# The first layer's weights and the dense work of both batches in one phase, the second batch's projections between the first one's feed-forward jobs

## The reference

```
xn = layernorm(x)
Q, K, V = (xn @ W.T).reshape(b, 16, t, 16) for W in (Wq, Wk, Wv)   # a plain reshape: 64 tokens make one head
x = x + softmax_causal(Q @ K.T / 4) @ V @ Wp.T + bp
      + rms_norm(relu(xn @ ternary(W_fc).T) ** 2) @ ternary(W_proj).T
# ternary(w): w rounded to bfloat16, in groups of 64; scale = mean |w| of a group,
# q = clip(round(w / scale), -1, 1), result q * scale. W_fc is 1024 x 256, W_proj 256 x 1024.
```

## Time and profile before

| | us |
|---|---|
| median of 3 runs | 1415.71 |
| lowest, highest | 1410.51, 1415.78 |
| the profiled execution: its time | 1415.78 |
| the profiled execution: its span | 1414.0 |

### The profile page before, as it was taken

How to read it: one execution, slowest core, us unless ns; L and a number is a source line. 1 busy time by engine, 2 the same in 40 slices (tenths; PEclk the granted TensorE clock), 3 DMA queues, 4 the chain that set the end, 5 groups by cost and what they waited for, 6 DMA issues and landing times. The chain is left out here.

```text
span 1414.0 us, 22409 instructions
## 1 busy us (share of the span) xinstructions
PE 1207.6 (85%) x7424; PEld 863.5 (61%) x7424; DVE 880.8 (62%) x2323; ACT 736.7 (52%) x1683; POOL 515.6 (36%) x545
## 2 busy tenths in 40 slices
PE   2584936899999898888589999999999999999978
PEld 2474834444444386776467767676776776766667
DVE  7674637989999534544476666666766666666501
ACT  1461610677877615545266566665666656666400
POOL 0130323433442100505055554545555554555200
PEclk8796975889999997999789999999999999999989
DMA  2262737446650093210311110110111111110091
GB/s 89 56 128 64 115 89 79 55 56 100 97 61 24 1 256 123 64 39 0 96 27 41 42 42 21 49 31 28 41 42 42 41 42 42 27 31 16 16 314 58
DMA packets 111100, 91.50 MB, mean 65 GB/s; under 512 B 49488, under 2 KB 101136, under 8 KB 109200
## 3 DMA queue, kind: packets, MB, share of 16 engines
q1 hardware_dynamic: 109952, 89.10, 27.8%
q10 hardware_dynamic: 1040, 1.05, 0.2%
HBM read 51.05 MB, written 30.67 MB: 58 GB/s over the span
## 5 line engine op out<-in xcount | busy, mean ns | idle before, releaser
L775 POOL TENSOR_SCALAR a_p<-a_p,a_rl 128x128 f32<-128x128 f32 (+7 forms) x256 | 216.3, 846 | 346.1 <-DVE a_rl L717 346.0
L758 ACT ACTIVATE a_p<-psum,a_nm 128x128 f32<-128x128 f32 (+7 forms) x256 | 189.5, 740 | 112.0 <-DVE a_nm L711 111.6
L1261 ACT ACTIVATE a_pt<-psum 128x512 f32<-128x512 f32 (+3 forms) x384 | 167.6, 493 | 73.1 <-PE psum L1121 70.5
L808 PE MATMUL psum<-ident,a_p 128*128 128x128 f32 x1152 | 171.3, 276 | 22.5 <-DVE a_pt L744 20.0
L830 PE MATMUL psum<-a_pt,v 128*64 128x256 f32 (+1 forms) x1280 | 160.3, 372 | 0.6 <-ACT a_ot L844 0.6
L1111 PE MATMUL psum<-a_op_k,a_op_q 64*128 64x512 f32 (+3 forms) x384 | 135.2, 449 | 27.7 <-DVE a_op_k L1227 26.5
L808 PEld LDWEIGHTS psum<-ident,a_p 128*128 128x128 f32 x1152 | 129.4, 141 | 46.3 <-issue 39.2
L711 DVE CUSTOM_DVE_ANT_0 psum<-psum,mask_a 128x128 f32<-128x128 f32 (+3 forms) x128 | 63.4, 496 | 139.3 <-PE psum L793 139.2
L1121 PE MATMUL psum<-a_op_q,a_op_k 64*128 64x512 f32 (+3 forms) x384 | 127.4, 411 | 8.4 <-ACT a_pt L1261 7.2
L742 ACT ACTIVATE a_pt<-psum 128x256 f32<-128x256 f32 (+2 forms) x192 | 87.2, 454 | 88.0 <-PE psum L808 86.9
L1121 PEld LDWEIGHTS psum<-a_op_q,a_op_k 64*128 64x128 f32 x384 | 62.4, 192 | 102.0 <-ACT a_pt L1261 83.2
(11 more groups left out here) (313 smaller groups left out, 2775.9 us busy)
## 6 DMA issues: line engine op xcount, KB each, us to landing
a_swap<-w_p SPq DMA_DIRECT2D x64, 128.0 KB, 2.4
ot_d<-a_ot SPq DMA_DIRECT2D x16, 512.0 KB, 2.6
o_ot<-ot_d SPq DMA_DIRECT2D x8, 1024.0 KB, 8.7
a_raw_q<-qk_d SPq DMA_DIRECT2D x48, 128.0 KB, 4.3
room<-qk_d SPq DMA_DIRECT2D x48, 128.0 KB, 7.6
w<-wf_d SPq DMA_DIRECT2D x16, 384.0 KB, 3.4
qk_d<-p_stage_h SPq DMA_DIRECT2D x64, 64.0 KB, 2.0
qk_d<-p_stage_l SPq DMA_DIRECT2D x64, 64.0 KB, 2.0
```

The costliest lines, as they stand in the source:

```text
L758: e.activation(s.p[:, t % NPB, 0:(i + 1) * P], C.score[t % 2][:, 0:(i + 1) * P], ACT.Exp, scale=-1.0, bias=s.nm[:, k:k + 1], accum_out=s.l ...
L775: e.tensor_scalar(s.p[:, t % NPB, 0:(i + 1) * P], s.p[:, t % NPB, 0:(i + 1) * P], s.rl[:, k:k + 1], 1.0, ALU.mult, ALU.mult).then_inc(s.no ...
L808: ins = e.transpose(C.turn[par][:, (k - k0) * P:(k - k0 + 1) * P], s.p[:, tt % NPB, k * P:(k + 1) * P], C.ident[:, :])
L1261: e.activation(pt[:, k // G0 % NPT, hd, off:HALF], bank_b("score", g, k)[:, off:HALF], ACT.Exp, scale=-1.0).then_inc(exped, 1)
```

## The change

`weights0`, `project0`, `feed0` and the loop over the batches go. One function, `dense0`, does their work for both batches in one phase, with an order written out by hand for each engine:

- SyncE loads batch 0's x, then Wq, Wk, Wv, Wp, W_proj, batch 1's x and the bias. ScalarE's queue still issues W_fc.
- The projection jobs of a batch are ordered qk, qk, v, four times. Batch 0's twelve run without lifts; between them VectorE quantises W_fc in eight steps (`Quantised`: narrow, magnitude, limits (two), below, above, sign, scaled, which are the instructions of `ternary`) and takes batch 1's layer-norm statistics. The transposes of W_fc and Wp come after job 7, those of batch 1's rows after job 11.
- Then 12 slots hold batch 1's projection n and batch 0's lift n. VectorE quantises W_proj in slots 2 to 7. Its transposes and batch 0's first drop follow slot 11.
- Then batch 0's lifts 12 to 15 and batch 1's 16 lifts run, with the drops spread between them, one token tile after a lift. Batch 1's second drop ends the phase.
- The bias is added to x on GpSimd, ahead of all squares, instead of on VectorE. The stage of Q and K holds two groups of 128 rows instead of four, and the stage of V, one tile, serves both batches. The rounded tiles h_h and h_l have 12 rooms instead of 16. The ring tiles r, h and sq first hold the weights.
- Batch 0's norm and additions are done within batch 1's lifts.

The diff, cut to its core (`Turns` has the units of transposes with their waits, `Rows0` the layer norm's steps):

```diff
-def weights0(nc, C, W, Wq, Wk, Wv, Wp, Wfc, Wproj):
...
-def project0(ph, C, W, b, x_in, xt_h, xt_l, x, qk_d, v_d, bias, bp):
...
-def feed0(ph, C, W, before, b, xt_h, xt_l, x, bias, acc_d):
...
+class Quantised:
...
+    def below(self, e):
+        e.wait_ge(self.step, 4)
+        lim = self.limit[:, :].unsqueeze(2).to_broadcast(self.shape)
+        e.scalar_tensor_tensor(out=self.neg[:, :, :], in0=self.wb[:, :, :], scalar=-1.0, in1=lim,
+                               op0=ALU.mult, op1=ALU.is_gt).then_inc(self.step, 1)
+
...
+JOBS_P = [job for mt in range(4) for job in (("qk", mt, 0), ("qk", mt, 1), ("v", mt, None))]
+JOBS_F = [(c, m) for c in range(NCH) for m in range(NH0)]
+N_P, N_F = len(JOBS_P), len(JOBS_F)
+ROOMS_H = 12
...
+def dense0(nc, C, w_p, x_in, weights, bp, qk_d, v_d, acc_d):
...
+        stage_h, stage_l = (ph.sb(f"stage_{n}", [P, 2, T], F32R) for n in "hl")
+        stage_v = ph.sb("stage_v", [P, NT // 2, 2 * E])
+        h_h, h_l = (ph.sb(f"h_{n}", [P, ROOMS_H, HALF], F32R) for n in "hl")
...
+        wfc, wpr, qfc = flat_h, flat_r, flat_r
+        qpr = xn[:, :, :].rearrange("p t e -> p (t e)")
...
+                load_x(0)
...
+                load_x(1)
+                e.dma_start(bias[:, :], bp.rearrange("(a m) -> a m", a=1).to_broadcast([P, E])).then_inc(bias_in, 16)
+                for b in range(B):
+                    for mt in range(4):
+                        J = b * N_P + 3 * mt + 2
+                        e.wait_ge(p_high, J)
+                        e.wait_ge(p_low, b * 8 + 2 * mt + 2)
+                        for part, stage in ((0, stage_h), (1, stage_l)):
+                            for j in range(P // D0):
...
+                    e.wait_ge(p_high, (b + 1) * N_P)
+                    e.dma_start(v_d[b * T:(b + 1) * T, :].rearrange("(t p) m -> p t m", p=P),
+                                stage_v[:, :, :].rearrange("p c (t m) -> p (c t) m", m=E)).then_inc(v_stored, 16)
...
+            @block.tensor
...
+                def project(b, n):
+                    kind, mt, c = JOBS_P[n]
+                    J = b * N_P + n
+                    bank = p_banks[J % 2]
+                    if J >= 2:
+                        e.wait_ge(p_high, J - 1)
+                        old_b, old_n = divmod(J - 2, N_P)
+                        if JOBS_P[old_n][0] == "qk":
+                            e.wait_ge(p_low, old_b * LOWS_P[N_P] + LOWS_P[old_n + 1])
...
+                def drop(b, c, i):
+                    if i == 0:
+                        e.wait_ge(high, b * N_F + (c + 1) * NH0)
+                        e.wait_ge(low, b * N_F + (c + 1) * NH0)
+                        if b:
+                            e.wait_ge(added, 4 * (c + 1))
...
+                e.wait_ge(loaded, 64)
+                for u in U["qkv"]:
+                    turns.turn(e, u)
+                for u in U["rows0"]:
+                    e.wait_ge(rows[0].made, 4 * ((u - U["rows0"][0]) // KE + 1))
+                    turns.turn(e, u)
+                turns.taken(e, "rows0")
+                for n in range(N_P):
+                    project(0, n)
+                    if n == 7:
+                        e.wait_ge(fc.made, 1)
+                        for u in U["fc"]:
+                            turns.turn(e, u)
+                        e.wait_ge(padded, KE + 1)
+                        for u in U["wp"]:
+                            turns.turn(e, u)
+                for u in U["rows1"]:
+                    e.wait_ge(rows[1].made, 4 * ((u - U["rows1"][0]) // KE + 1))
+                    turns.turn(e, u)
+                turns.taken(e, "rows1")
+                for n in range(N_F):
+                    if n < N_P:
+                        project(1, n)
+                    lift(0, n)
+                    if n == N_P - 1:
+                        e.wait_ge(pr.made, 1)
+                        for u in U["pr"]:
+                            turns.turn(e, u)
+                        turns.taken(e, "pr")
+                        for i in range(4):
+                            drop(0, 0, i)
+                e.wait_ge(p_high, B * N_P)
+                e.wait_ge(p_low, B * LOWS_P[N_P])
+                square_sums(0, 0)
+                for n in range(N_F):
+                    lift(1, n)
+                    if n in (2, 3, 4, 5):
+                        drop(0, 1, n - 2)
+                    if n == 3:
+                        square_sums(0, 1)
+                    if n in (10, 11, 12, 13):
+                        drop(1, 0, n - 10)
+                    if n == 11:
+                        square_sums(1, 0)
+                drop(1, 1, 0)
+                square_sums(1, 1)
+                for i in range(1, 4):
+                    drop(1, 1, i)
+            @block.scalar
...
+                        if M >= 2:
+                            e.wait_ge(stored[M % 2], (M // 2) * 16 * 2 * (P // D0))
...
+                        if b:
+                            e.wait_ge(v_stored, 16 * b)
...
+                def round_h(N):
+                    e.wait_ge(squared, N + 1)
+                    if N >= ROOMS_H:
+                        e.wait_ge(down, dropped(N - ROOMS_H))
...
+                rows[0].root(e)
+                for u in [*U["qkv"], *U["rows0"]]:
+                    turns.round_high(e, u)
+                for n in range(N_P):
+                    project(0, n)
+                    if n == 7:
+                        for u in [*U["fc"], *U["wp"]]:
+                            turns.round_high(e, u)
+                    if n == 8:
+                        rows[1].root(e)
+                for u in U["rows1"]:
+                    turns.round_high(e, u)
+                for N in range(B * N_F):
+                    if N < N_P:
+                        project(1, N)
+                    cut(N)
+                    if N >= 2:
+                        round_h(N - 2)
+                    if N == N_P - 1:
+                        for u in U["pr"]:
+                            turns.round_high(e, u)
+                    if N == N_F + 5:
+                        mean_root(0)
+                for N in range(B * N_F - 2, B * N_F):
+                    round_h(N)
+                mean_root(1)
+            @block.gpsimd
+            def _(e):
+                def add_bias(b):
+                    e.wait_ge(rows[b].made, NT)
+                    for tt in range(NT):
+                        e.tensor_tensor(x[b][:, tt, :], x[b][:, tt, :], bias[:, :], ALU.add).then_inc(biased, 1)
+                e.wait_ge(bias_in, 16)
+                for b in range(B):
+                    add_bias(b)
...
+            @block.vector
...
+                for n in range(NT // 2):
+                    rows[0].count(e, n)
+                rows[0].variance(e)
+                rows[0].rows(e)
+                for u in [*U["qkv"], *U["rows0"]]:
+                    turns.keep_low(e, u)
+                fc.narrow(e)
+                pr.narrow(e)
+                project(0, 0)
+                fc.magnitude(e)
+                project(0, 1)
+                fc.limits(e)
+                fc.below(e)
+                fc.above(e)
+                project(0, 3)
+                fc.sign(e)
+                project(0, 4)
+                fc.scaled(e)
+                e.wait_ge(loaded, 64)
+                e.memset(wpp[:, :, :, :], 0.0).then_inc(padded, 1)
+                project(0, 6)
+                e.wait_ge(padded, 1)
+                for mt in range(KE):
+                    e.tensor_copy(wpp[:, mt, :, 0:D0], wp[:, mt, :].rearrange("p (h d) -> p h d", d=D0)).then_inc(padded, 1)
+                rows[1].count(e, 0)
+                rows[1].count(e, 1)
+                project(0, 7)
+                rows[1].count(e, 2)
+                rows[1].count(e, 3)
+                rows[1].variance(e)
+                project(0, 9)
+                turns.all_turned(e, "rows0")
+                rows[1].rows(e)
+                project(0, 10)
+                for u in U["rows1"]:
+                    turns.keep_low(e, u)
+                quantise = {2: pr.magnitude, 3: pr.limits, 4: pr.below, 5: pr.above, 6: pr.sign}
+                for N in range(B * N_F + 2):
+                    if N < N_P:
+                        project(1, N)
+                    if N >= 2:
+                        join(N - 2)
+                    if N in quantise:
+                        quantise[N](e)
+                    if N == 7:
+                        turns.all_turned(e, "rows1")
+                        pr.scaled(e)
+                    if N == N_F + 5:
+                        means(0)
+                    if N == N_F + 7:
+                        add(0)
+                means(1)
+                add(1)
...
-            with ExitStack() as dense:
...
-                bias = dsb("bias", [P, E])
-                with nc.Fori(0, B) as b:
-                    with Phase(nc, "d0", repeated=True) as ph:
```

(40 more changed lines are left out.)

527 lines of the change are left out of this document (241 added, 286 removed).

## The result

| | before | after |
|---|---|---|
| median, us | 1415.74 (4 runs) | 1394.65 (4 runs, 1392.24 to 1401.04) |
| profiled execution: time, span | 1415.78, 1414.0 | 1393.61, 1391.8 |
| mean granted clock | 0.923 | 0.937 |
| first instruction of the next phase | 203.22 | 184.30 |

The ratio is 0.9852, with an interval of 0.9816 to 0.9888: 1.5% faster. The forecast was 1385; its range held the time, and its own smaller range (1374 to 1395) just did. The profiled executions differ by 22.2 us: 18.9 of them lie ahead of the next phase, 3.3 behind it. Forecast were 30.4 and 0.

The account below looks back on a forecast made before the run. TensorE bounds only the slots; other stretches are chains through VectorE, GpSimd and DMA. Stage end points put the next phase at 172.8 instead of 203.2 us: 1415.78 less 30.4 gives 1385 us, range 1369 to 1401 (own 1374 to 1395).

Parts of the forecast that it names:

- Start: From phase start to the first projection, through loads, rows and transposes: 21.5 us, where it was 57.66 before.
- Batch 0's projections: Batch 0's projections beside W_fc's quantising, then batch 1's rows and transposes: to 55 us.
- V's wait: ScalarE at batch 1's first V job stands from 61 until batch 0's V store lands at 65.9: cost 4.9 us.
- Slots: Twelve slots, paced by VectorE without pause from the first join at 68.2, with 10.8 us of W_proj's steps: to 97.5.
- First drop: W_proj's transposes (3.66 us, plus 0.6 for ScalarE), then batch 0's first drop of 64 matmuls (7.54 us): to 109.3.
- Twenty lifts: Lifts with eight token tiles of drops, paced by GpSimd and VectorE at 2.1 us a unit: 50 us, to 159.3.
- End: Last drop at the lower clock 9.1 us, fourth powers 0.5, one addition 0.5, then 3.4 to the next phase: 172.8.
- Rival 1: In the lifts, squares fit beside VectorE's work and TensorE paces: 13.5 us less, 1372; chance 0.15.
- Rival 2: In the slots, Q/K and V stores on SyncE's queue pace through the two-group stage: +12 us, 1397; chance 0.16.
- Rival 3: From 21 us on, TensorE falls to the lower clock and stays there: +46 us, 1431, slower than before; chance 0.06.
- Rival 4: Time is moved, not saved: the next phase starts early but loses as much; within 0.5% of now; chance 0.03.
- three conditions under which I would be wrong: Lifts 1.8 us apart; ScalarE's Q/K store waits over 3 us in sum; lower clock in over half of 21 to 160 us.

Follow-up runs that it names:

- short quantising: Changed kernel with three of W_proj's quantising steps left out (both comparisons and their difference), so output differs: 1390.89 us, ratio 0.9831 to the kernel before.
- late drops: Changed kernel with the two drops between batch 1's lifts begun two lifts later, 14 rooms for h_h and h_l: 1390.2 us, ratio 0.9844 to the kernel before.

## Why the prediction was right in sign and 10 us short

**Start (21.5; measured 22.59), right.** The bias additions on GpSimd took 7.54 us for eight (0.94 each, beside the casts) and 5.54 (0.69 each): inside 0.5 to 1.0. One cast went from 1.22 to 1.77 us, the hindrance that I had put at 0.5.

**Batch 0's projections (55; measured 53.3, batch 1's first stage on ScalarE at 55.30), right.** The sum, the comparisons and the product took 2.27 to 2.29 us as read in the earlier trace rows, and VectorE had no wait over 0.2 us from 24 to 44 us. The one term left out is the stage's wait at 46.10, 1.20 us.

**V's wait (4.9; measured 5.63, ending at 66.00 where I had 65.9), right as a wait, not as a price.** Without it the first join came 6.3 us earlier, but join 9 only 3.5 and the phase's end 2.1. In the sum I priced it as if nothing were late behind it, though the store of Q and K was next in line, with waits of 3.46 and 1.44 us.

**Slots (first join 68.2, measured 67.64; end 97.5, measured 96.2 by the last matmul of lift 11), right, for the reason given.** VectorE has no idle from join 0 to join 8 and the short quantising shows that it paces. The rule that I weighed here (the Trainium skill, SBUF — State Buffer, section "SBUF: two separate sides") foresaw exclusion for the quantising too, at +2 us. Part of that is seen: a square begun beside a comparison took 1.96 or 2.50 us instead of 1.04, and one beside the product 1.78. But the comparison kept its 2.28, so GpSimd paid and VectorE, which paces, did not:

```profile
80.49 2.28 DVE L400 TENSOR_TENSOR d_wb_pr<-d_wb_pr,d_limit_pr 128x2048 bf16<-128x2048 bf16 x1
...
81.17 2.50 POOL L717 TENSOR_TENSOR d_h<-d_r 128x512 f32<-128x512 f32 x1 [1.15 <-ACT d_r L657]
```

Beside the sum, which has one input, the square kept its 1.04 (69.17).

**First drop (to 109.3; measured 107.8, the next low part at 109.92), right.** The 16 transposes ran at the full clock, 1.91 us for my 3.66, and ScalarE's rounding behind them took TensorE 1.92 us for my 0.6.

**Twenty lifts (50; measured 61.7, 107.8 to 169.5), wrong, and this is the step that failed.** The failed term is "2 for the lifts held back behind a drop that waits for the eighth low part". The terms for VectorE and GpSimd were right and somewhat high: from join 10 on VectorE is busy for 41.0 of 59.6 us (2.05 a unit where the pair is closed, 1.20 where the squares were made before) against 46.4 for them and the norm. Its idle time is 18.6 us instead of 2. I priced the wait by its length on one engine. But it is a round trip: behind the low part waited for, VectorE has one more join, and the next unit is rounded only behind a ReLU whose lift stands behind the token tile. So the other engines run dry while TensorE catches up on a whole tile, cold. The two waits cost about 9 us (late drops: 8.9 less idle). At the full clock, in the same order, they would cost 4.1 less (matmuls ahead of the drops: 2.87 and 2.83 instead of 4.57 and 5.20). Most of the other 9.7 is TensorE's 2.83 us a unit, larger than the pair's 2.1. I had TensorE's 35.2 us and the pair's 44.4 as two totals and took the larger; stage by stage the larger one changes.

**End (13.5 from the last low part; measured 14.8, 169.5 to 184.30), about right.** It ran cold as forecast, behind 5.95 us of idle TensorE. Of the eight additions two were left for the end, not one: 0.88 us at 180.34.

**Behind the phase (0; measured −3.3).** Nothing there was changed. The attention phase took 288.8 us against 288.5, and the difference came in the dense phase after it. The two spread by 6.6 and 6.4 us between executions of kernels that share them, so no cause is named. It hides a part of the miss by luck: the phase ended 11.5 us later than forecast, the profiled execution 8.2.

**The rivals.** Rival 1 (the pair doesn't pace) fell: 2.05 us with the square on GpSimd, 1.80 without. Rival 2 (stores) was wrong as built but right as what is next: 3.46 us with V's store first, 4.55 with the projections in one piece. Rival 3 (the lower clock) held in places and not throughout. The clock was 0.94 in 22.6 to 53.6 us with TensorE busy for 24.13 of 31.0, and its lowest stretches, 0.68 and 0.50, lie right behind waits of 5.6 and 6.1 us. The sum never came near the 30 us that turn the sign. What the Trainium skill (TensorE: Matmul & The Clock Gate, section "A second HAM failure mode: psum-queue depth-cycling") says of short idling that cycles the clock is not seen in that row. Rival 4 did not come: the phase's gain stays.

The three conditions under which I would be wrong were not met, but one sign failed: the next phase's first instruction came at 184.30, not at 168 to 178. In the bursts the joins came 2.05 us apart or more, except where their squares were made before (1.20); the ReLUs ran ahead of them within the ring at 1.52. Over all 22 joins from 109.92 a unit took 2.7. The waits for Q/K stores sum to 1.2 us, and the mean granted clock from 22 to 160 us is 0.89, that is some fifth of the time at the lower level.

## What to carry to other kernels

When reductions are spread between producers on an in-order engine, place each so that what it waits for is several units old, and look at each in-order queue for what then stands behind it; a reduction that waits for a new unit can drain every engine behind it. The lower clock after the wait cost 4 us where the others had run dry, and little where they had units in hand. Compare the engines' totals stage by stage, because each stage has its own largest. And a wait that is taken away is worth what separates it from the next wait in line: here 3.5 us were left at join 9 of the 6.3 won at the first join.

## What was not expected of the hardware

- The issues of small stores slow down beside a large one on the same queue: eight of 64 KB took 3.72 and 3.76 us, then 6.07 and 5.14 right behind V's 1 MB store.
- GpSimd's square of 128x512 (1.04 us alone) took 1.96 and 2.50 us beside VectorE comparisons of 128x2048 bf16, which kept 2.28, and 1.04 us beside the one-input sum of that size; beside a float32 low part both stretch (1.27 and 1.52 against 1.04 and 0.68).
- An unchanged phase of 288.5 us took up to 295.1 in another execution of a kernel that has it word for word.
